# The low half of a feed-forward intermediate, moved from GpSimd to the vector engine

## What is computed

```python
x = x + layernorm(attention(layernorm(x), Wq, Wk, Wv, Wo))
x = x + layernorm(ffn(layernorm(x), gate_cp, up_cp, down_cp))

# ffn: three dense weights are interpolated from short lists of control points
gate = einsum('bsh,ih->bsi', h, gate_w)      # 512 -> 2048
up = einsum('bsh,ih->bsi', h, up_w)
inter = silu(gate) * up
return einsum('bsi,hi->bsh', inter, down_w)  # 2048 -> 512
```

## Time and profile before

| what | value |
|---|---|
| median of 3 runs | 875.4 us (872.71 to 875.8) |
| the profiled execution's own time | 878.51 us |
| its span, first to last instruction | 876.6 us |
| busy: TensorE, VectorE, ScalarE, GpSimd | 87%, 60%, 42%, 51% |
| feed-forward block | from about 424 us to the end |
| mean granted TensorE clock | 0.931 of full |

### The profile page before, as it was taken

One profiled execution on the slowest core, in us unless ns is written; L12 is line 12 of the kernel. 1 busy time (PEld: TensorE's weight loads), 2 busy tenths in 40 slices (PEclk: granted clock), 3 DMA queues, 4 the chain that ended last, 5 costly groups with the idle time before them and its releaser, 6 DMA issues.

```text
span 876.6 us, 19208 instructions
## 1 busy us (share of the span) xinstructions
PE 764.5 (87%) x7152; PEld 514.7 (59%) x7152; DVE 525.6 (60%) x1025; ACT 369.9 (42%) x632; POOL 446.5 (51%) x616
## 2 busy tenths in 40 slices
PE   5696899999999998998485999979879799798996
PEld 3574667786778776776232555645546456464565
DVE  6562853685368534656364667757567577673553
ACT  3330333243234322323354646646456465564641
POOL 4399449744974487014143444544445355354542
PEclk9798799999999999899587998989989899898998
DMA  8345347513751375118706053262542623516122
GB/s 295 127 157 165 106 132 241 170 48 124 249 170 48 121 251 131 33 45 273 257 13 228 3 172 131 90 213 74 164 139 74 210 92 119 171 59 220 49 63 73
DMA packets 64313, 120.54 MB, mean 138 GB/s; under 512 B 12144, under 2 KB 28656, under 8 KB 62192
## 3 DMA queue, kind: packets, MB, share of 16 engines
q1 hardware_dynamic: 64240, 119.53, 41.4%
HBM read 82.94 MB, written 36.57 MB: 136 GB/s over the span
## 4 chain that ended last, share of the span: by engine, by line
PE 26%; SPq 10%; DMA 5%; DVE 4%; ACT 3%; issue 3%; POOL 0%; ACTq 0%; DVEq 0%
SPq L885 8%; PE gbank L1401 5%; PE ubank L1401 4%; PE ybank L1440 3%; DMA token_features<-z_lo 3%; PE ybank L1442 2%; PE ybank L1441 2%; PE mbank L1415 2%; DMA out<-x_res 1%; ACT gated L1237 1%; PE turned L960 1%; PE ybank L1429 1%; DVE inter L1304 1%; ACT act L1233 1%; PE ybank L1431 1%
## 5 line engine op out<-in xcount | busy, mean ns | idle before, releaser
L1192 POOL TENSOR_TENSOR act<-inter,act 128x512 f16<-128x512 f32 x128 | 158.2, 1245 | 177.2 <-ACT act L1233 177.2
L1304 DVE SCALAR_TENSOR_TENSOR inter<-ubank,c_up,gated 128x512 f32<-128x512 f32 x128 | 95.9, 749 | 91.4 <-ACT gated L1237 86.6
L1440 PE MATMUL ybank<-down,act 128*128 128x160 f16 x512 | 112.8, 239 | 0.0
L1441 PE MATMUL ybank<-down,act 128*128 128x160 f16 x512 | 112.2, 238 | 0.0
L1442 PE MATMUL ybank<-down,act 128*128 128x160 f16 x512 | 112.2, 238 | 0.0
L1237 ACT ACTIVATE gated<-gbank,c_gate 128x512 f32<-128x512 f32 x128 | 87.8, 686 | 57.7 <-PE gbank L1401 57.6
L1233 ACT CAST act<-inter 128x512 f16<-128x512 f32 x128 | 78.9, 616 | 47.4 <-DVE inter L1304 47.4
L1401 PE MATMUL gbank<-z,s_twice 128*32 128x512 f16 x512 | 55.1, 421 | 44.8 <-ACT gated L1237 29.6
L1440 PEld LDWEIGHTS ybank<-down,act 128*128 128x128 f16 x512 | 50.9, 99 | 41.8 <-issue 38.0
L1401 PEld LDWEIGHTS gbank<-z,s_twice 128*32 128x32 f16 x512 | 13.3, 94 | 73.4 <-ACT gated L1237 35.7
L1401 PE MATMUL ubank<-z,s_twice 128*32 128x512 f16 x512 | 53.7, 410 | 2.5 <-DVE inter L1304 2.5
(11 more groups left out here) (190 smaller groups left out, 2111.8 us busy)
## 6 DMA issues: line engine op xcount, KB each, us to landing
x_ln<-x SPq DMA_DIRECT2D x64, 256.0 KB, 3.4
z<-token_features SPq DMA_DIRECT2D x16, 1024.0 KB, 6.2
job<-job_in SPq DMA_DIRECT2D x24, 640.0 KB, 5.2
shared<-x SPq DMA_DIRECT2D x32, 256.0 KB, 2.7
x<-shared SPq DMA_DIRECT2D x32, 256.0 KB, 2.0
token_features<-z_hi SPq DMA_DIRECT2D x64, 128.0 KB
token_features<-z_lo SPq DMA_DIRECT2D x64, 128.0 KB
x_res<-x SPq DMA_DIRECT2D x32, 256.0 KB, 2.7
```

Source lines behind the costliest of these rows:

```text
L1192: pool.tensor_tensor(hidden[par][:, i, TOK:2 * TOK], inter[:, i % INTERS, :], hidden[par][:, i, 0:TOK], ALU.subtract).then_inc(inter_ready, 1)
L1304: dve.scalar_tensor_tensor(out=inter[:, i % INTERS, :], in0=ubank[:], scalar=c_up[:], in1=gated[:, i % 2, :], op0=ALU.mult, op1=ALU.mult). ...
L1440: pe.matmul(out, hidden[par][:, r, high], box[:, 0], start=False, stop=False)
L1441: pe.matmul(out, hidden[par][:, r, high], box[:, 1], start=False, stop=False)
```

## The change

GpSimd's function `low` is taken away. VectorE gets one of the same content, and calls it in every step directly behind `product`: in step n it makes `product` of n + 2 and then `low` of n + 1. It waits there for ScalarE's cast of n + 1. `product` no longer waits for the low half of four steps earlier, since that now stands ahead of it on the same engine. At the start `low` of step 0 stands between `product` 0 and `product` 1.

```diff
         @block.gpsimd
         def _(pool):
-            def low(n, i, par):
-
-                pool.wait_ge(inter_hi_done, held(pool, n + 1))
-                pool.tensor_tensor(hidden[par][:, i, TOK:2 * TOK], inter[:, i % INTERS, :], hidden[par][:, i, 0:TOK],
-                                   ALU.subtract).then_inc(inter_ready, 1)
-
...
                     n = g * I + i
-                    if not (isinstance(n, int) and n == STEPS - 1):
-                        low(n + 1, (i + 1) % I, par if i + 1 < I else 1 - par)
...
             feats.scale(pool, Q + 1)
-            low(0, 0, 0)
             feats.scale(pool, Q + 2)
...
                 dve.wait_ge(silu_done, n + 1)
                 dve.wait_ge(up_done, n + 1)
-                if not (isinstance(n, int) and n < INTERS):
-                    dve.wait_ge(inter_ready, n - INTERS + 1)
                 dve.scalar_tensor_tensor(out=inter[:, i % INTERS, :], in0=ubank[:], scalar=c_up[:],
                                          in1=gated[:, i % 2, :], op0=ALU.mult, op1=ALU.mult).then_inc(inter_done, 1)
+
+            def low(n, i, par):
+
+                dve.wait_ge(inter_hi_done, n + 1)
+                dve.tensor_tensor(hidden[par][:, i, TOK:2 * TOK], inter[:, i % INTERS, :], hidden[par][:, i, 0:TOK],
+                                  ALU.subtract).then_inc(inter_ready, 1)
...
                     if not (isinstance(n, int) and n >= STEPS - 2):
                         product(n + 2, i + 2)
+                    if not (isinstance(n, int) and n == STEPS - 1):
+                        low(n + 1, (i + 1) % I, par if i + 1 < I else 1 - par)
...
             product(0, 0)
+            low(0, 0, 0)
             product(1, 1)
```

## The result

| what | before | after |
|---|---|---|
| median of 4 runs each, us | 874.06 (871.67 to 875.8) | 897.7 (895.51 to 901.75) |
| ratio, 95% interval | | 1.0278 [1.0231, 1.0325] |
| the profiled execution's own time, us | 878.51 | 895.51 |
| its span, us | 876.6 | 893.7 |
| mean granted TensorE clock | 0.931 | 0.945 |

The change costs 23.6 us by the medians, 24.3 by the ratio; 20.0 were forecast, as 895.4 us in a range of 884 to 903.

The account below looks back on a forecast made before the run. Engines pace TensorE's restart to first spill issue, then SP's queue and transfers. Delays by `low` sum to 2.9 + 17.4 - 0.3 = 20.0 us, 898.5 from the profiled 878.5; the runs' median is 3.1 lower, so 895.4, range 884 to 903.

Parts of the forecast that it names:

- seven first pieces: Stretches from TensorE's restart behind a spill to the next spill's first issue; forecast to grow by 20.3 us in all.
- the second interval: Second of the seven stretches from TensorE's restart to the first spill issue; about 3.1 us of cost claimed.
- The price: Each `low` on VectorE delays what stands behind it by 0.60 us, bounds 0.54 and 0.75, without waiting for the cast.
- the relief of `x_res`: On VectorE, without GpSimd's `low` beside it, `x_res` takes 0.75 us instead of 1.62, 0.87 less.
- The clock in the new gaps: TensorE's granted clock was expected to stay up in its new waits of 1 to 1.6 us.
- the first interval: First of the seven stretches, in group 0 without output work; fewer operations but more exposed ones, 2.9 us claimed.
- the interval that was worked through: From 582.9 to 619.65 us, quads 3, 0 and 1 up to the spill: 0.28 + 1.60 + 1.20 = 3.1 us.
- second pieces: From the first spill issue to TensorE's next restart, set by SP's queue and the transfers; no change claimed.
- Stall and tail: TensorE's stall before the restart shrinks by about 1 us; the end gains 0.3 us from a dropped wait for `low`.
- Lows in gaps: Rival, about 884 us: only quad 0's gaps pass the delay on, 1.2 us in each of seven intervals; chance 0.11.
- VectorE as the bound: Rival, about 914 us: VectorE can't use its gaps, so a whole group's 16 `low` count; chance 0.10.
- Faster: Rival, about 870.7 us: shorter `x_res` lets SP's queue spill earlier, 4.7 us less with the end; chance 0.04.

Follow-up runs that it names:

- the repetition: The changed kernel run again without an edit, in more rounds, against the kernel before: 896.74 us against 874.39, ratio 1.0247.
- The halves by steps: Two kernels with 64 of 128 `low` on VectorE, the rest on GpSimd, against before: steps 2 and 3 ratio 1.0034, steps 0 and 1 ratio 1.0217.
- the kernel with the gaps: All 128 `low` on VectorE, but placed in its gaps instead of directly behind `product`, against the kernel before: 873.29 us against 874.62, ratio 0.9985.
- the kernel with the quiet `x_res`: The kernel before, with GpSimd's `low` of step 2 waiting until VectorE has finished that step's output tile: 871.13 us against 875.18, ratio 0.996.
- The second dose: The changed kernel with each subtraction made a second time into an unread tile, 256 on VectorE: 934.66 us against 875.18 for before, ratio 1.0683.

## Why the prediction was right, point by point

- **Direction and size.** Right: 20.3 us in the seven first pieces, as summed. By the medians the cost is 23.6, and 22.4 in the repetition, so the forecast lies slightly low. That the two sums agree to a tenth is in part luck: the second interval cost 1.3 us more than forecast, the first and the third 0.5 and 0.7 less, and the rest cancel.
- **The price.** 0.60 us in place of its neighbour, 681 ns in duration, no wait for the cast: as forecast. The rule of the Trainium skill's page "VectorE: DVE Perf Modes" (Two Vector instructions with no wait between them) let the overlap stand, since all tiles start in the same quarter; the spacing of 0.60 at a duration of 0.68 agrees.
- **Where it lies on the path.** The order of the terms held: TensorE's waits in quad 0 are 1.56 and 0.81 us (forecast 1.6 and 0.8) and 0.85 in quad 1 (about 1). The chain through the first spill issue, after, passes through the two `z_lo` and not through `x_res`:

```profile
628.24 1.29 DVE z_lo L946 x2
...
629.55 0.60 SPq L885
```

  The halves by steps and the kernel with the gaps show it by runs: 19.0 us for the subtractions ahead of `h_lo` and `hT`, 3.0 for the others, and no net cost when all lie in gaps; the last two are net of the relief of `x_res`.
- **Terms mis-sized, within a first piece.** Two, of opposite sign. `products` of quad 3 did wait for `hT`, 0.51 us, where the slack was to leave 0.28; it came out at 0.25 on the path because TensorE was sooner at the full clock (below). The second interval cost 4.38 us where about 3.1 was forecast, and there the clock took most of the excess. Timeline of TensorE in group 0, quad 3, in before and then after:

```profile
478.42 0.61 PE L960 MATMUL turned<-ident,h_hi 128*128 128x128 f16 x4 [0.74 <-DVE h_lo L935]
...
482.07 0.23 PE L972 MATMUL zbank<-hT,feat 128*128 128x128 f16 x1
```

```profile
479.02 0.61 PE L960 MATMUL turned<-ident,h_hi 128*128 128x128 f16 x4 [1.34 <-DVE h_lo L935]
...
482.67 0.29 PE L972 MATMUL zbank<-hT,feat 128*128 128x128 f16 x1
```

  Both restart at 475.8. The wait for `h_lo` takes its 0.60. But `products` then take 0.22 us each in before, and up to 0.32 after; the 24 of them last 1.45 us (482.07 to 483.52) against 2.44 (482.67 to 485.11). The windows of 481.8 to 483.8 us, in before and then after, with the columns as above:

```profile
481.80:483.80 2.00, 2.00 (x36) 1.52 (x36) 0.36 (x1) 0.62 (x1) 1.47 (x2) 0.93 0.00 0
```

```profile
481.80:483.80 2.00, 2.00 (x23) 1.16 (x16) 1.57 (x3) 0.62 (x1) 0.55 (x2) 0.50 0.00 0
```

  TensorE was granted its full clock at about 482 us before, and at about 484.7 after: 1.0 us of the excess of 1.3. The repetition has the same (its matmuls of `products` at 0.31 us). The longer wait looks like the reason, but its length alone does not decide. The same place, TensorE in group 0, quad 3, with steps 0 and 1 on VectorE and then with steps 2 and 3:

```profile
481.61 0.61 PE L960 MATMUL turned<-ident,h_hi 128*128 128x128 f16 x4 [1.34 <-DVE h_lo L935]
...
485.24 0.22 PE L972 MATMUL zbank<-hT,feat 128*128 128x128 f16 x1
```

```profile
477.66 0.61 PE L960 MATMUL turned<-ident,h_hi 128*128 128x128 f16 x4 [0.74 <-DVE h_lo L935]
...
481.60 0.31 PE L972 MATMUL zbank<-hT,feat 128*128 128x128 f16 x1
```

  With the wait of after, 1.34 us, `products` run at 0.22 us; with the wait of before, 0.74, they run at 0.31. The kernel that makes each subtraction twice waits 1.94 us and has 0.22. Counted from the restart, the full clock came back after 5.8 to 8.4 us in the six profiles with a wait of 0.74 us (6.3 in before), after 6.4, 9.0 and 9.3 in the three with 1.34 (the last two are the changed kernel's), and after 7.3 with 1.94. So the 1.0 us is not shown to be a cost of the change; whether the longer wait helped to delay the clock in its two profiles stays open.
- **The clock in the new gaps.** The prediction expected that it stays up. In one place it did not: in group 0, quad 1, the wait for `h_lo` grew from 1.23 us to 1.83, and a few matmuls behind it the duration of one rose from 0.40 us to 0.62. Timeline of TensorE after:

```profile
449.81 0.40 PE L960 MATMUL turned<-ident,h_hi 128*128 128x128 f16 x4 [1.83 <-DVE h_lo L935]
...
450.95 0.62 PE L1399 MATMUL ubank<-z,s_twice 128*32 128x512 f16 x4
```

  The granted clock is 0.67 from 450 to 452, 0.50 from 452 to 454 and 0.98 behind that; the repetition has the same dip, and before, the kernel with the gaps and the one with the quiet `x_res` have none behind this wait. Its price is not separated from the rest: the first interval as a whole cost 2.39 us, less than the 2.9 forecast, and before ran it at 1.2 GHz up to about 444 us, from its own restart. In the gaps of the interval that was worked through the clock stayed up.
- **`x_res`.** The relief came in full and everywhere, 0.746 us on average, as the port rule of the Trainium skill's page "SBUF — State Buffer" (SBUF: two separate sides) has it: an operation of VectorE with two SBUF inputs and one of GpSimd exclude each other for a whole instruction. It was right for four of the seven spills that `z_lo` decides after the change (the issue follows its end within 0.1 us); in the other three SP arrives 1.58, 1.48 and 0.46 us behind `z_lo`, where the prediction had two. The relief was mis-sized: `x_res` took 1.32 us on average before and not 1.62, so it gave back 0.58 us each and not 0.87. Its way through SP's queue is as described, and with nothing else changed it gave 3.5 us: in before SP comes 0.19 to 2.24 us behind `z_lo` in five of the seven spills, in the kernel with the quiet `x_res` 0.03 to 0.8.
- **What paces the second pieces.** "SP's queue and the transfers set it" was half wrong: with a quarter of the issues taken off the queue the stretch did not shrink. What lies behind the queues sets it; what that is stays open. The forecast didn't hang on it, since the change moves no transfer.
- **Stall and tail.** The stall went from 4.57 to 3.82 us (forecast 1 less). The 0.34 us wait of the earlier trace rows is gone, but the next one, for `mom_lo`, grew from 0.54 to 1.62 us, so the end gained only 0.1 of the 0.3 forecast. Timeline of TensorE at the end, before and then after:

```profile
850.41 0.39 PE L1429 MATMUL ybank<-down,mom_hi 128*128 128x512 f16 x1 [0.54 <-DVE mom_lo L1310]
```

```profile
867.86 0.39 PE L1427 MATMUL ybank<-down,mom_hi 128*128 128x512 f16 x1 [1.62 <-DVE mom_lo L1305]
```

- **Busy time.** VectorE rose by 56 us, not by 65: 87.1 for `low` less 18 for `x_res` (1.32 to 0.75 us, 32 times) is 69, but busy time counts an overlap once, and each `low` that runs up to its neighbour overlaps it by 0.08 us (0.68 less 0.60), which by this estimate is up to 10 us for 128 and most of the missing 13. GpSimd fell by 157 (forecast 158).
- **The rivals.** Lows in gaps (884) and VectorE as the bound (914) are outside the interval of the result. Faster (870.7): its mechanism, the shorter `x_res`, is real, 3.5 us against some 25 for the subtractions (21.6 and 3.5); it comes to the surface where the subtractions lie in gaps, or stay on GpSimd.

What single profiles can't settle is the last 3 us: the profiled execution of before was 4.5 us above its median, so the 20.3 may be some us too small, and the first pieces of the kernel with the quiet `x_res` (238.1 us, 8.5 less than before's, where its runs give 3.5) stand too far below it.

## What to carry to other kernels

Work taken from an engine that nobody waits for bought nothing by itself here, whatever its idle time and its price there; what it costs on the new engine is the spacing of its instructions, only where something critical is queued behind them without a gap. So put such work behind the last critical instruction of a stage, or into the wait of a chain over two engines (`norm`, cast, `feats.low`), and not directly behind the instruction that makes its input: here the place was worth 2.6%, and the engine nothing that the runs can tell (0.9985). When a free engine's operation meets one of VectorE that reads two SBUF tiles, look at the shortest and the median duration of the latter first: keeping the two apart by a wait (0.996) was at least as good as moving the work into gaps (0.9985), and simpler.

## What the runs showed of the hardware

- **TensorE's level at a restart.** In before all seven restarts behind a stall begin with a matmul of 0.62 us (the 1.2 GHz level), at stalls of 2.87 to 6.46 us. In after four of seven begin with 0.40 us (the 2.4 GHz level), at stalls of 2.05 to 3.82, and in the kernel with the gaps five of seven, at 2.16 to 4.19. Within those ranges both were seen: 3.67 us gave 0.62 in after. At 589.92 the full level lasted for two matmuls and fell at 590.70, but then the full clock was back 4.1 us after the restart (0.97 granted from 593.9 to 595.9), against 5.0 in before (0.75 from 586.9 to 588.9). These are single executions; which level a restart finds is not tied to the kernel by them.
- **When the full clock comes back.** In group 0, quad 3, it took between 5.8 and 9.3 us from the restart in ten profiles, and the length of TensorE's first wait there (0.74 to 1.94 us) did not order them.
- **Issues that get longer.** With four of 16 issues off SP's queue several of the others took up to 1.5 us, where 0.57 to 1.20 stood in before, and the 16 together took as long, at 179 GB/s against 180.
- **The second dose costs more than the first:** 36 to 38 us against 22 to 24 for 128 subtractions, as the gaps fill.
